# A two-layer decoder on one core: mask added by a matmul, ten expert slots, a re-timed plan and fill matmuls in every stage

## What is computed

```python
x = x + L0_attn(ln(x))     # rms norm, a = sigmoid(xA+b), h = sigmoid(xC) * scan(a, sigmoid(xD) * xB), out
x = x + L0_xattn(ln(x))    # 16 heads over 64 context rows, boolean mask, softmax
x = x + L0_ffn(ln(x))      # one linear map and a low-rank one
x = x + L1_attn(ln(x))     # LSTM of 20 cells over 512 steps; it places a Gaussian window over the past rows
x = x + L1_xattn(ln(x))    # as L0_xattn, integer mask, softmax then times group_prob
x = x + L1_ffn(ln(x))      # 8 experts, each token goes to the one with the highest logit
```

## Time and profile before

| | us |
|---|---|
| median of 3 runs | 3188.12 |
| the runs | 3192.34, 3178.17, 3188.12 |
| the profiled execution, its own time | 3191.33 |
| its span, first to last instruction | 3189.5 |
| mean granted clock of TensorE | 0.847 |

### The profile page before, as it was taken

One profiled execution on the slowest core, in us unless ns is written; L12 is line 12 of the kernel. 1 busy time (PEld: TensorE's weight loads), 2 busy tenths in 40 slices (PEclk: granted clock), 3 DMA queues, 4 the chain that ended last, 5 costly groups with the idle time before them and its releaser, 6 DMA issues.

```text
span 3189.5 us, 39732 instructions
## 1 busy us (share of the span) xinstructions
PE 2584.9 (81%) x11385; PEld 1542.6 (48%) x11385; DVE 1893.2 (59%) x6517; ACT 853.2 (27%) x2341; POOL 1317.4 (41%) x1372
## 2 busy tenths in 40 slices
PE   5799896977778778778778787999998868887945
PEld 3466453543636354635354545544544535544533
DVE  4576787768685767586768686645655414242311
ACT  0233242332232233223232332212222212122211
POOL 0363342324443345334444453423432545555534
PEclk9999896978786887678878786999899889899965
...
GB/s 160 54 62 13 49 12 38 1 71 14 48 24 39 33 53 25 58 20 58 20 57 20 57 14 47 34 41 34 33 40 36 71 119 90 127 96 100 27 92 81
DMA packets 195337, 164.88 MB, mean 52 GB/s; under 512 B 52913, under 2 KB 188171, under 8 KB 194896
## 3 DMA queue, kind: packets, MB, share of 16 engines
...
...
## 4 chain that ended last, share of the span: by engine, by line
PE 36%; issue 21%; DVE 19%; POOL 12%; DMA 6%; SPq 3%; ACT 2%; POOLq 0%; DVEq 0%; ACTq 0%
PE p L775 4%; PE p L869 4%; PE p L832 4%; PE p L808 4%; PE p L769 3%; DVE l_xnat L1185 3%; PE p L786 3%; DMA out<-xy,xid 3%; DMA xw<-in_w_proj 3%; PE p L822 2%; POOL l_scratch L1547 2%; PE pg L841 2%; DVE ln_stats L1160 2%; PE p L849 2%; POOL l_scratch L1542 2%
## 5 line engine op out<-in xcount | busy, mean ns | idle before, releaser
L1521 POOL TENSOR_TENSOR ln_rstd<-ln_ve,neghalf 128x4 f32<-128x4 f32 x96 | 98.2, 1023 | 714.6 <-DVE ln_ve L1169 713.2
L1535 POOL TENSOR_TENSOR l_kbd<-l_kg,headmask 128x512 f32<-128x512 f32 x256 | 266.8, 1052 | 305.5 <-PE p L808 210.7
L1465 DVE SCALAR_TENSOR_TENSOR uin<-gates 16x20 f32<-16x20 f32 x512 | 175.5, 343 | 283.4 <-ACT gates L987 281.5
L832 PEld LDWEIGHTS p<-l_vg,l_scratch 128*128 128x128 f32 x2048 | 282.2, 215 | 75.0 <-issue 36.6
L987 ACT ACTIVATE gates<-pg 16x80 f32<-16x80 f32 x512 | 114.9, 224 | 761.0 <-PE pg L841 759.4
L1542 POOL TENSOR_TENSOR l_scratch<-l_scratch,l_mx 128x512 f32<-128x512 f32 x256 | 265.3, 1042 | 117.5 <-DVE l_mx L1215 116.7
L832 PE MATMUL p<-l_vg,l_scratch 128*128 128x34 f32 x2048 | 292.7, 296 | 15.9 <-ACT l_scratch L1016 6.8
L769 PE MATMUL p<-ident,l_xnat 128*128 128x128 f32 x1024 | 202.0, 339 | 123.2 <-DVE l_xnat L1185 122.0
L841 PE MATMUL pg<-wcat,slots 128*16 128x80 f32 x1024 | 177.2, 260 | 150.9 <-DVE slots L1477 149.0
L808 PE MATMUL p<-l_kbd,l_qT 128*128 128x512 f32 x512 | 275.6, 628 | 10.9 <-DVE l_scratch L1211 9.7
L841 PEld LDWEIGHTS pg<-wcat,slots 128*16 128x16 f32 x1024 | 59.0, 97 | 387.9 <-DVE slots L1477 238.5
...
## 6 DMA issues: line engine op xcount, KB each, us to landing
...
xw<-in_w_fc SPq DMA_DIRECT2D x84, 128.0 KB, 2.2
xw<-in_w_proj SPq DMA_DIRECT2D x84, 128.0 KB, 2.5
...
```

The source lines that it names most:

```text
L832: i = pe.matmul(o_bank[l][:, q * VW:(q + 1) * VW], w.exT[:, j, p, :], w.vg[:, b, q * VW:(q + 1) * VW], start=True, stop=True)
L1465: dve.scalar_tensor_tensor(uin[:, :], gates[:, 0:20], 1.0, gates[:, 60:80], ALU.add, ALU.mult)
L1535: pool.tensor_tensor(w.kbd[b % 2][:, j, :, :], w.kg[:, j, b:b + 1, :].broadcast_to([P, NE, SK]), headmask[:, :].rearrange("p (a o) -> p a ...
```

## The change

Five things are changed together.

1. **Attention.** `mask` and `shift` go. The queries are scaled by -0.25, so that the bank holds minus the scores; before each `score` matmul PE multiplies an identity (`same`, bf16) with `neg` (now bf16, of the other sign), which puts the mask into the bank, and the score matmul adds to it. `max` becomes a minimum read from PSUM. `exp` becomes eight ACTIVATEs of 128x64, one a head, that read PSUM with scale -1 and the head's minimum as a bias from SBUF, in four planned steps of two. The bank is now held until the last of them (`score` waits for `exped` of u - 2).
2. **Durations** of the plan, and `HOPS`.
3. **Spread** of the LSTM: no longer a number for each stage; the planner tries 72 to 144 in steps of 8 and keeps the plan that ends first.
4. **Fills** in all stages. In stages 1 to 3 they write partitions 64 to 127 of the LSTM's bank.
5. **Experts**: 10 slots for weights and tokens, laid over the weights and lane-0 tiles that are no longer used by then, and 4 for results; tiles are loaded in pairs; `TILE_EVERY` 3.5 becomes 2.8, the DMA delay of the plan 3.0 becomes 7.0.

```diff
-TILE_SLOTS = 4
+TILE_SLOTS, OUT_SLOTS = 10, 4
...
-            ("pool", "keys", u, 1.0, [("score", u - 4)]),
-            ("pe", "score", u, 0.85, [("qland", u % 2), ("keys", u), ("mask", u - 2)]),
-            ("dve", "mask", u, 0.6, [("score", u), ("neg", 0), ("pturn", u - 4)] + ([("rows", 3)] if u == 0 and ahead else [])),
-            ("dve", "max", u, 0.6, [("mask", u)]),
-            ("pool", "shift", u, 1.0, [("max", u)]),
-            ("act", "exp", u, 0.5, [("shift", u)])]
+            ("pool", "keys", u, 1.07, [("score", u - 4)]),
+            ("pe", "score", u, 1.1, [("qland", u % 2), ("keys", u), ("neg", 0), ("exp", 4 * (u - 2) + 3)]),
+            ("dve", "max", u, 0.65, [("score", u), ("exp", 4 * (u - 4) + 3)] + ([("rows", 3)] if u == 0 and ahead else []))]
+        steps += [("act", "exp", 4 * u + e, 0.45, [("max", u), ("pturn", u - 4)])
+                  for e in range(4)]
...
-        steps += [("pe", "gates", s, 0.15, [("state", s - 1), ("slots", s // 8)]), ("act", "tanh", s, 0.15, [("gates", s)]),
-                  ("dve", "cell", s, 0.35, [("tanh", s)]), ("act", "tcell", s, 0.15, [("cell", s)]),
-                  ("dve", "state", s, 0.35 if s % 8 < 7 else 0.75, [("tcell", s)])]
+        steps += [("pe", "gates", s, 0.34, [("state", s - 1), ("slots", s // 8)]), ("act", "tanh", s, 0.23, [("gates", s)]),
+                  ("dve", "cell", s, 0.5, [("tanh", s)]), ("act", "tcell", s, 0.15, [("cell", s)]),
+                  ("dve", "state", s, 0.4 if s % 8 < 7 else 0.75, [("tcell", s)])]
...
-HOPS = {"pe": 0.22, "act": 0.2, "dve": 0.18, "pool": 0.1, "sp": 0.2, "dma": 3.0, "clock": 0.0}
+HOPS = {"pe": 0.15, "act": 0.08, "dve": 0.08, "pool": 0.1, "sp": 0.2, "dma": 7.0, "clock": 0.0}
-PACE = {0: (0.0, 4.0, 0.4), 1: (96.0, 16.0, 0.6), 2: (128.0, 4.0, 0.3), 3: (140.0, 0.0, 0.4), 4: (112.0, -18.0, 0.35),
-        5: (0.0, 22.0, 0.4), 6: (0.0, 0.0, 0.4)}
+PACE = {0: (4.0, 0.4), 1: (16.0, 0.6), 2: (4.0, 0.3), 3: (0.0, 0.4), 4: (-18.0, 0.35), 5: (22.0, 0.4), 6: (0.0, 0.4)}
-TILE_EVERY = 3.5
+TILE_EVERY = 2.8
-IDLE, FILL, WARM = 0.3, 0.9, (0, 4, 5)
+IDLE, FILL, WARM = 0.3, 0.9, (0, 1, 2, 3, 4, 5, 6)
...
+    spreads = range(72, 152, 8) if 1 <= stage <= NC_ else (0,)
+    return min((planned_at(stage, ahead, spread) for spread in spreads), key=lambda plan: plan[0])[1]
...
+            ("clock", "due", p, 2 * every, [("due", p - 1)]),
+            ("sp", "mload", p, 5.6, [("due", p - 1), ("mexpert", 2 * p + 1 - TILE_SLOTS), ("mscatter", 2 * p + 1 - TILE_SLOTS)]),
...
-            ("sp", "mload", k, 1.5, [("due", k - 1), ("mexpert", k - TILE_SLOTS), ("mscatter", k - TILE_SLOTS)]),
...
+                    pe.matmul(banks[l][j], same[:, :], w.neg[:, b:b + 1, :].broadcast_to([P, NE, SK]), start=True, stop=False)
                     pe.wait_ge(t.kbd, N + 1)
                     pe.matmul(banks[l][j], w.qT[:, j, b * P:(b + 1) * P],
-                              w.kbd[b % 2][:, j, :, :].rearrange("p a k -> p (a k)"), start=True, stop=True
+                              w.kbd[b % 2][:, j, :, :].rearrange("p a k -> p (a k)"), start=False, stop=True
...
+                    if 1 <= layer < NC_:
+                        pe.matmul(pg[64:128, :], warm[:, 0:64], warm[:, :], start=True, stop=True)
...
+                    for h in (2 * e, 2 * e + 1):
+                        i = act.activation(w.ex[b % 2][:, NE * j + h, :], banks[lane][j][:, h * SK:(h + 1) * SK], ACT.Exp, scale=-1.0,
+                                           bias=w.mx[:, u % 4, h:h + 1])
...
-                    dve.tensor_tensor(w.ex[b % 2][:, heads, :], banks[l][j].rearrange("p (a k) -> p a k", a=NE),
-                                      w.neg[:, b:b + 1, :].broadcast_to([P, NE, SK]), ALU.add).then_inc(t.masked, 1)
...
+                    dve.tensor_reduce(w.mx[:, u % 4, :], banks[l][j].rearrange("p (a k) -> p a k", a=NE), AX_X, ALU.min).then_inc(t.top, 1)
...
-                    pool.tensor_tensor(ex, ex, w.mx[:, i_ % 4, :].rearrange("p (a o) -> p a o", o=1).broadcast_to([P, NE, SK]),
-                                       ALU.subtract).then_inc(t.shifted, 1)
...
+            def load_experts(first):
+
+                for q in (first, first + 1):
+                    s = q % TILE_SLOTS
+                    if q >= TILE_SLOTS:
+                        sp.wait_ge(m_expert, q - TILE_SLOTS + 1)
+                        sp.wait_ge(o_store[(q - TILE_SLOTS) % OUT_SLOTS], 16 * ((q - TILE_SLOTS) // OUT_SLOTS + 1))
```

212 lines of the change are left out of this document (107 added, 105 removed).

## The result

The kernel after takes 2884.39 us (median of four runs, 2873.20 to 2891.23), the kernel before 3190.23 beside it (3178.17 to 3193.20): a ratio of 0.9044 with a 95% interval of 0.9007 to 0.9082. That is 306 us saved where 510 were forecast, 204 us above the 2680, and 34 us above the end of the range, 2850. The profiled execution is the fastest of the four: 2873.2 us, span 2871.3.

The account below looks back on a forecast made before the run. The middle was taken as bound by a chain of some 155 us a body, partly on a slow clock, stage 4 by the plan, stages 5 and 6 by expert tiles. 92 + 248 + 325 + 1069 + 400 + 360 + 81 + 105 = 2680 us; range 2540 to 2850.

Parts of the forecast that it names:

- Rival B: Attention: ACT becomes the bound, exps without overlap, 3.0 us a half-step; 2885 us, or 2780 in half of them; chance 0.10.
- ACT takes POOL's place and nothing is won there: Stage 0 attention: ACT's 2.2 us a half-step replaces POOL's 2.1, so no gain within attention; stage 0 253 to 248.
- beside the wait for the bank: Mask matmuls on PE: 0.23 us each, 3.7 us a body, most of it hidden beside that wait.
- I take 162 a body, so that DVE is 81% full: Stage 1: two bodies fall from 371 to 325 us; bounds 148 and 178 a body.
- 17 us a body for the clock: Stages 2 and 3: fills raise the clock to 0.97, saving 7 us in attention and 10 us on the chain.
- 9 us for a lighter DVE queue in truer order: Stages 2 and 3: 10.9 us less DVE work and a queue ordered by true durations save 9 us a body.
- The sign that the forecast had set for this: Middle bodies above 150 us at a full clock would show the chain is not PE's and the prediction wrong.
- lower bound, 12 us a body: Stages 2 and 3: least saving, attention and a third of the clock, where 26 us a body was forecast.
- not all at one end together: Whole kernel: the forecast's own range from its terms' bounds, taken as not all failing alike, 2550 to 2800 us.
- C: Stages 1 to 3: lanes and LSTM still hinder each other, bodies save only 10 us; 2834 us; chance 0.17.
- D: Stages 5 and 6: experts don't speed up, SP's queue still waits for pairs and weights; 2848 us; chance 0.07.
- E: Stages 1 to 3: fills delay real work, kernel slower; at clock 0.65, 198 us a body, about 3320 us; chance 0.04.

Follow-up runs that it names:

- run 9: Kernel after with 4 slots and 2 result slots for the experts in place of 10 and 4: 3120.50 us.
- run 8: Kernel after without the spread search, with the old spreads 96, 128, 140 and 112 in stages 1 to 4: 2952.34 us.
- run 7: Kernel after with the old planned durations (experts, score and exp steps excepted), old HOPS except the DMA's, and old spreads: 2996.52 us.
- run 6: Kernel after with the attention of before: mask on DVE, shift on POOL, one exp, no mask matmul: 2962.55 us.
- run 3: Kernel after with FILL 0.5 for 0.9 in all stages, 1292 fills for 2727: 2841.98 us.
- run 13: Kernel after with other PACE numbers and FILL 0.25, 393 fills: 2889.82 us.
- run 4: Kernel after with one exp of 512 columns in place of eight of 64, without subtracting the row's maximum: 2850.14 us.
- run 5: Kernel after without the 256 mask matmuls, so both masks are left out: 2846.40 us.
- run 14: Kernel after with other PACE numbers and FILL 0.5, but stage 0 ordered by the old durations, HOPS and PACE: 2789.24 us.
- run 2: Kernel before with fills added in stages 1 to 3 and nothing else changed: 3132.38 us.
- run 10: Kernel after with a longer LSTM step, two unread ACTIVATEs added in each: 2886.84 us.
- run 11: Kernel after with a longer landing, two unread 128x512 ACTIVATEs added at each landing of a norm's turned rows: 2995.29 us.
- run 1: Kernel after with no fill matmuls in stages 1 to 3: 2906.46 us.
- run 12: Kernel after with other PACE numbers and FILL 0.5, the search then taking other spreads in stages 2 and 3: 2799.24 us.

## Why the prediction was right and wrong

- **The experts' slots (right).** Stage 5 at 121 us a body against 120, stage 6 at 109 against 105; run 9 shows the cause as far as the slots go. SP's wait did not go wholly (41 us are left, 279 before).
- **Stage 4 (right).** 98 us a body against 100. The spread gives 12 of 18 us (run 8), the true durations 3.1 more (run 7 against run 8), and the new attention 7.5 (run 6), which I had not counted there; the three overlap.
- **The clock is held by the fills (right), the fills cost nothing (right for the bodies).** 0.96 to 1.00 against 0.97 taken; run 3 moves no body by over 1 us. What I missed is that half of them, at 0.93 to 0.95, give the same time, and that a quarter do not (run 13).
- **ACT's exp (right).** The timeline of ACT in the kernel after (start, length, count, idle before):
```profile
160.19 1.33 ACT L1034 ACTIVATE l_scratch<-p,l_mx 128x64 f32<-128x64 f32 x6 [0.70 <-DVE l_mx L1234]
```
Six take 1.33 us, 0.21 from one to the next (1.33 less the last one's 0.29, by five). Rival B had 0.31 and fell with it; that ACT's share would then set the body is not borne out either, as run 4 takes 17 us of ACT out of a stretch and gains nothing. The Trainium skill (ScalarE: Activation LUTs, what ACT_TABLE_LOAD costs) gives 280 ns + 0.833 ns a column with an overlap of 93 ns between neighbours, so an estimate of 0.24 us for 64 columns. The trace has 0.21, and that page's budget of 0.3 us for each ACTIVATE in its rules for kernel authors, which I had weighed, is too high here, as it leaves the overlap out.
- **Stage 0 (wrong, +26 us).** The step that failed: "ACT takes POOL's place and nothing is won there". I asked which of POOL and ACT is fuller, when the earlier trace rows say that PE is busy 35.00 of 35 us at a clock of 1.00. PE was the bound, and I had put 16 mask matmuls on it and costed them as lying "beside the wait for the bank", where there was no wait. Run 5 gives 2.2 us a body for them, run 6 5.4 us for the whole new attention. The rest of the 10 us is an order made worse by better durations: 4.6 us with the old attention, 6.7 with the new (runs 6, 7 and 14). I had not counted any price of a new order.
- **Stage 1 (wrong, +33 us).** "I take 162 a body, so that DVE is 81% full" rests on a share, with no wait named that would go. That is the step that failed: the body is 179.7 us, with DVE 75% full. In run 2 the clock went to 0.99 and the body stayed at 183. The planner's own end for this body is 173.7 us by the true durations, and no body of the table is more than 5 us below the end that its planner had (the run without the mask matmul apart); so the plan alone spoke against 162. Runs 10 and 11 say that the LSTM's and layer 0's chains are both on it. Which wait would have to go first stays open, and so does whether another order would be better: runs 1, 3 to 5 and 8 to 14 all have the kernel after's in stage 1, and the three others, in runs 2, 6 and 7, are slower (183.3, 184.3 and 187.6).
- **Stages 2 and 3 (wrong, +108 us).** The steps that failed are the forecast's 17 us a body for the clock (7 and 10) and its 9 us for a lighter DVE queue in truer order: together 26, and the stages give (1277 - 1177) / 8 = 12.5. The sign that the forecast had set for this, bodies above 150 us at a full clock, did not come (they are at 147 and 144), but these two steps fell short all the same. Of the 17 run 1 shows 1.4 in stage 2 and 6.8 in stage 3. Of the 9, the new attention gives 5.5 in stage 2 and nothing in stage 3 (run 6), and the true durations alone -3.4 and 6.9 (run 7 against run 8). (The working also priced the clock up to 1.00, not up to the 0.97 taken; that is 29.2 us of PE's work for 26.5, and changes little.) In stage 2 the gain went into waits between engines that the order sets, and with another order (runs 12 and 14) its body is at the 134 forecast. In stage 3 that is not shown: no order tried gets below 143, and run 11 lengthens layer 0's chain and is paid in full. What would have to change there, and which steps stood in the wrong place in stage 2, stays open.
- **The range.** Stages 2 and 3 came out at their lower bound, 12 us a body (14 by the working's own words, 7 and a third of 20.8), and stage 1 just beyond its own, 179 for 178. With every bound at its bad end the terms give 2923 us. The range left that out, as "not all at one end together". But one cause, the order that the planner happens to make, stands behind the clock's worth, DVE's and stage 1's, so these terms could well fail together, and did.
- **Rivals.** C said 10 us a body in stages 1 to 3 and 2834 in all; the bodies saved 4, 11.5 and 11.1. That is near the case that came, with stage 0 on top, which no rival had. D and E were far off: stages 5 and 6 are within 4 us of their terms, and the lowest clock of a stage is 0.92. E's own point was too high by its own numbers, since two of its ten bodies take 185 us already and not 160: about 3270 us for 3320.
